# Attention and mixture kernel: VectorE takes the second key tile's turned probabilities out of PSUM

## What is computed

```
h = layernorm(x)
q = rope(rms_norm(h) * q_norm_w)          # 16 heads of width 32
k = rope(rms_norm(ctx) * k_norm_w)        # 4 key heads, each for 4 query heads
v = ctx                                   # 4 value heads
s = where(causal, q @ k.T / sqrt(32), -1e30)
x = x + softmax(s) @ v @ w_out.T
y = layernorm(x)
probs = softmax(y @ w_router); the 4 largest of 128 give each of 8 bases a weight per token
mixed = sum over 8 bases of weight * silu(y @ w_gate) * (y @ w_up)
x = x + mixed @ w_down + (silu(y @ shared_gate) * (y @ shared_up)) @ shared_down
```

## Time and profile before

| | |
|---|---|
| device time, median of 3 runs | 809.68 us (809.2 to 809.68) |
| the profiled execution's own time | 809.42 us |
| its span | 807.7 us |
| TensorE busy | 763.8 us, 95% |
| VectorE busy | 646.1 us, 80% |
| ScalarE busy | 578.0 us, 72% |
| GpSimd busy | 532.5 us, 66% |

### The profile page before, as it was taken

How to read it: one execution, slowest core, us unless ns; L and a number is a source line. 1 busy time by engine, 2 the same in 40 slices (tenths; PEclk the granted TensorE clock), 3 DMA queues, 4 the chain that set the end, 5 groups by cost and what they waited for, 6 DMA issues and landing times. The chain is left out here.

```text
span 807.7 us, 15292 instructions
## 1 busy us (share of the span) xinstructions
PE 763.8 (95%) x4180; PEld 608.0 (75%) x4180; DVE 646.1 (80%) x1635; ACT 578.0 (72%) x1413; POOL 532.5 (66%) x685
## 2 busy tenths in 40 slices
PE   2768799999999999999999999999999999999998
PEld 2545577777777878777778778777778887788886
DVE  7767787889788877889788787888788887688774
ACT  3878796788777867788778767787777775655552
POOL 4586489784697769775687849777465615662572
PEclk9979999999999999999999999999999999999999
DMA  8323144554545446545455445554545335454650
GB/s 291 122 68 97 41 134 161 179 166 138 192 156 172 153 141 220 194 154 178 146 175 179 141 157 181 170 164 135 197 150 173 136 125 185 157 188 133 207 201 35
DMA packets 57052, 127.03 MB, mean 157 GB/s; under 512 B 10920, under 2 KB 28040, under 8 KB 56968
## 3 DMA queue, kind: packets, MB, share of 16 engines
q1 hardware_dynamic: 56968, 126.04, 47.3%
HBM read 107.55 MB, written 4.46 MB: 139 GB/s over the span
## 5 line engine op out<-in xcount | busy, mean ns | idle before, releaser
L1634 PE MATMUL u<-w_h,t_h 128*128 128x512 f32 x640 | 258.4, 404 | 1.1 <-issue 0.8
L1634 PE MATMUL u<-w_l,t_h 128*128 128x512 f32 x640 | 251.2, 393 | 0.0
L1634 PE MATMUL u<-w_h,t_l 128*128 128x512 f32 x640 | 251.0, 392 | 0.0
L1284 DVE TENSOR_TENSOR w_l<-w_raw,w_h 128x512 fp32r<-128x512 f32 x288 | 240.4, 861 | 0.3 <-ACT w_h L945 0.3
L945 ACT ACTIVATE w_h<-w_raw 128x512 fp32r<-128x512 f32 x384 | 219.0, 621 | 7.9 <-DMA w_raw<-in_w_units 7.0
L899 POOL TENSOR_TENSOR w_l<-w_raw,w_h 128x512 fp32r<-128x512 f32 x96 | 139.1, 1449 | 101.8 <-ACT w_h L945 101.8
L980 ACT ACTIVATE scores<-scores,mx 128x384 f32<-128x384 f32 (+1 forms) x224 | 128.8, 575 | 70.4 <-DVE mx L1227 69.2
L907 POOL TENSOR_TENSOR macc<-macc,gb 128x256 f32<-128x256 f32 x112 | 106.1, 951 | 58.9 <-DVE gb L1387 58.4
L1634 PEld LDWEIGHTS u<-w_h,t_l 128*128 128x128 f32 x640 | 120.6, 188 | 26.9
L1227 DVE CUSTOM_DVE_ANT_0 scores<-s,mask_qk 128x384 f32<-128x384 f32 (+1 forms) x224 | 112.4, 503 | 35.5 <-PE s L1510 34.9
L1634 PEld LDWEIGHTS u<-w_h,t_h 128*128 128x128 f32 x640 | 121.0, 189 | 25.8 <-issue 3.0
(11 more groups left out here) (152 smaller groups left out, 1175.0 us busy)
## 6 DMA issues: line engine op xcount, KB each, us to landing
w_raw<-in_w_units SPq DMA_DIRECT2D x160, 512.0 KB, 4.2
w_raw<-in_w_out_t SPq DMA_DIRECT2D x16, 512.0 KB, 5.1
w_raw<-in_shared_w_down SPq DMA_DIRECT2D x16, 512.0 KB, 4.6
q_st<-turned_h SPq DMA_DIRECT2D x224, 32.0 KB, 2.8
out<-x SPq DMA_DIRECT2D x16, 256.0 KB, 2.2
q_st<-turned_l SPq DMA_DIRECT2D x112, 32.0 KB, 2.7
x<-in_x SPq DMA_DIRECT2D x3, 1024.0 KB, 9.2
k_st<-turned_h SPq DMA_DIRECT2D x48, 32.0 KB, 2.8
```

The costliest lines, as they stand in the source:

```text
L1284: e.tensor_tensor(w_l[:, i % WR, k, :], w_raw[:, i % WR, k, :], f32(w_h[:, i % WR, k, :]), ALU.subtract).then_inc(s_wl, 1)
L1634: last = e.matmul(u_bank[n % 2][:], t[:, k, cols], ww[:, i % WR, k, :], start=(k == 0 and m == 0), stop=(k == KC - 1 and m == 2))
```

## The change

In spans 0 to 3 the copy of the second key tile (`k = 1`, 512 columns) goes from ScalarE's queue to VectorE's, as `probabilities_out`, with a semaphore of its own, `s_exv`. It waits for the same transposes. All that waited for the copy (the value product, the next transposes into `pair`) waits for the new semaphore in those four cases. The copies of the first key tile and those of all later spans stay on ScalarE, which now counts four steps fewer.

```diff
+        def exp_out(u, k):
+
+            if u < KV:
+                return (s_exv, u + 1) if k else (s_ex, u + 1)
+            return s_ex, step_no(u, k) - KV + 1
+
         def probable(u, k):
             first = span(u)[1] * TH
             if u < KV or k < first:
-                return s_ex, step_no(u, k) + 1
+                return exp_out(u, k)
...
# GpSimd, mask_probabilities
-                e.wait_ge(s_ex, n + 1)
+                e.wait_ge(*exp_out(u, k))
...
# ScalarE, loop over slots
-                if (step := second_pass_step(s)) is not None:
+                if (step := second_pass_step(s)) is not None and not (step[0] < KV and step[1]):
                     exponential(*step)
...
# VectorE
+            def probabilities_out(u, k):
+                n, width = step_no(u, k), G * (Q - seen(u, k))
+                e.wait_ge(s_pb, n + 1)
+                if n >= PR:
+                    e.wait_ge(s_pv, n - PR + 1)
+                e.tensor_copy(pr[:, n % PR, 0:width], pair[:, 0:width]).then_inc(s_exv, 1)
...
# VectorE, loop over slots
                 for u in value_block(s):
                     attended(u)
+                if (step := second_pass_step(s)) is not None and step[0] < KV and step[1]:
+                    probabilities_out(*step)
                 for g in moments_in(s):
                     moments(g)
...
# TensorE, turn_probabilities and pass_b
-                p_free[0] = (s_ex, step_no(u, k) + 1)
+                p_free[0] = exp_out(u, k)
```

More of the change, by code:

```diff
@@ L226, in attention_and_mixture_kernel @@
             "row_inverse", "inverse_spread", "inverse_turned", "inverse_out"))
-        s_pb, s_ex, s_sel, s_pv = (sem(n) for n in ("pass_b", "exp", "exp_masked", "value_product"))
+        s_pb, s_ex, s_exv, s_sel, s_pv = (sem(n) for n in ("pass_b", "exp", "exp_out_dve", "exp_masked", "value_product"))
         s_att, s_oh, s_ol = sem("attended"), sem("out_high"), sem("out_low")
```

## The result

| | before | changed |
|---|---|---|
| device time, median of 12 runs each | 809.47 us (807.14 to 810.5) | 811.22 us (810.59 to 813.35) |
| ratio, with 95% interval | | 1.0033 (1.0023 to 1.0042) |
| span of the profiled execution | 807.7 us | 809.7 us |
| VectorE busy | 646.1 us | 647.4 us |
| ScalarE busy | 578.0 us | 576.6 us |

The changed kernel is 0.33% slower, 2.7 us (1.9 to 3.4) by the ratio of runs taken side by side, 1.75 us by the two medians. The forecast was 811.7 us, so 2.3 over the profiled execution of before. The changed kernel's median of 811.22 us lies just under the 811.3 that the prediction took as the border to slower; the ratio of runs side by side, whose whole interval lies above 1.002, tells it clearly.

What follows compares the result with a forecast made beforehand. From 30 to 62 us waits between engines bound the kernel, from 100 us TensorE. Steps 1.45 + 0.55 - 0.1 + 0.4 gave +2.3 us over the profiled 809.42, so 811.7 us; range 809.4 to 813.4.

Steps and rivals of the forecast that it cites:

- place 2: Span 1's copy, 39 to 41 us: it runs ahead of the row maximum, lateness grows from 1.45 to 2.0 us.
- place 1: Span 0's copy, 31 to 36 us: copy of 0.66 and moments of 0.88 us make the row maximum 1.45 us late.
- place 3: Span 2's copy, 47 to 50 us: maximum 3.1 us late, but slack at keys and turned_l leaves 1.9 us.
- place 4: Span 3's copy, 58 us: it runs ahead of the row maximum, lateness grows from 1.9 to 2.3 us.
- The copy's price: One 128x512 copy on VectorE: taken as 0.66 us, between ScalarE's 590 ns and the row maximum's 687 ns.
- its second case: Rival, chance 0.27: only the late start of SyncE's query transfers counts, +1.05 us, time 810.5 us.
- The value products: Span 0, sixteen products of 1.51 us at half clock: may fall in a better stretch, taking 0.3 to 0.6 us away.
- the range's first case: VectorE's waits at the four copies delay all behind them: +2.3 us, spanning 1.4 to 2.8 us; chance 0.48.
- ScalarE's relief at nothing: The 2.4 us of copies taken off ScalarE gain nothing, since in spans 0 to 2 it waits next for VectorE.
- the faster case: Rival, chance 0.13: ScalarE decides, each copy gives back up to 590 ns; one gives -0.6 us, all four -2.4 us.
- Carried one for one to the end: From 100 us on TensorE is the bound, so the 2.3 us of delay at 59 us stays to the end.
- The clock: Rival, chance 0.12: more waiting brings TensorE more time at 1.2 GHz, about +1.7 us on top, 813.4 us.

Runs made afterwards that it cites:

- experiment 3: From the changed kernel: each copy on VectorE stands behind the moments of its slot, not ahead of them; 810.84 us, ratio 1.0015 to before.
- experiment 7: From the kernel before: VectorE only waits for the transposes and writes one element of an existing tile, ScalarE keeps the copies; 809.79 us, ratio 1.0005.
- experiment 10: From the changed kernel: only span 0's copy is on VectorE, ScalarE has the other three; 809.80 us, ratio 1.0005 to before.
- experiment 1: From the changed kernel: the four copies are on no engine, value products read the first key tile's probabilities (wrong output); 809.13 us, ratio 0.9992 to before.
- experiment 4: From the changed kernel: each copy one slot later in VectorE's queue, behind the next row maximum and ahead of the inverse; 809.88 us, ratio 1.0008 to before.
- experiment 8: From the kernel before: span 3's queries turned three slots earlier, their transfers right behind; 810.73 us, ratio 1.0016 to before.
- experiment 6: From the changed kernel: the copies of spans 1 to 3 on VectorE, that of span 0 back on ScalarE; 810.61 us, ratio 1.0020 to before.
- experiment 2: From the kernel before: VectorE waits for the transposes and writes 8 elements of a new scratch tile, ScalarE keeps the copies; 813.57 us, ratio 1.0051.

## Why the prediction held

**The mechanism** was a wait put into VectorE's queue ahead of work that others need, and it is what the runs show up to 61 us. Its marks, forecast and found: row maximum behind the first copy 34.05, 33.75; first `q_st` transfer 34.9, 34.62; inverse 35.15, 34.85; maximum of place 2 41.45, 41.45; its inverse 42.5, 42.54; third copy 49.0, 49.07; maximum behind it 50.5, 50.51; first maximum over 384 51.7, 51.76; `turned_l` 52.2, 52.24; last maximum 60.6, 60.29; exponential 61.3, 61.02.

Some of this agreement is luck. The changed kernel's profiled execution was 0.63 us early when the first copies began (its first wide copy at 30.01, that of before at 30.64), and its first transposes then took 1.09 in place of 0.63 us. By the steps, which don't know of the start, the sum stands as follows; place 1 between executions with transposes of the same length, the others as means of two executions each:

| place | forecast | steps, changed - before |
|---|---|---|
| 1 | +1.45 | 8.51 - 6.87 = +1.64; 9.00 - 7.51 = +1.49 |
| 2 | +0.55 | 8.23 - 7.63 = +0.60 |
| 3 | -0.1 | 10.64 - 10.82 = -0.18 |
| 4 | +0.4 | 3.15 - 2.78 = +0.37 |
| sum | +2.3 | +2.3 to +2.4 |

That the sum agrees to 0.1 us is luck as well: step 1 is known to some 0.2 us, and step 3 was 11.06 and 10.57 in the two executions of before, 10.64 in both of the change.

**The copy's price** was taken as 0.66 us and has two values. It is 692 ns long, just above the upper of the two bounds (687), but the next instruction of VectorE starts 0.60 to 0.61 us behind the start of it (32.30 to 32.91, 40.84 to 41.45, 49.07 to 49.67), near the lower (590). What stands behind it feels the second; of the 0.3 us by which the maximum of place 1 came early, 0.2 were there when the copy started. By the table in the Trainium skill (VectorE: DVE Perf Modes, The TRN2 errata) the estimate was 658 ns, between the two; no row here is that long.

**Place 1** was forecast as copy plus moments. Experiments 3, 7 and 10 show both halves: moments first takes it away (6.97), the wait without the copy keeps 0.96 of 1.49, alone it is there in full. In the changed kernel the transfers weren't what passed it on, as the prediction said against its second case: the first maximum over 384 elements, which had waited 0.73 us for TensorE, starts right behind the inverse (51.76). They weren't far off: with place 1 alone TensorE waited 0.96 us for a transfer before 52.80 us.

**Place 2** by the length of the copy holds, and so does **place 3** absorbed by the wait for keys and transfers: with the copy ahead of the last maximum step 3 was 10.38 to 10.78 us in four executions, in the two of before 10.57 and 11.06. The -0.18 of the table is less than that scatter.

**The value products** of place 1 were a term at the low side of the range: 1.51 us as the price of the lower clock, against 0.86, with 0.3 to 0.6 us to be had in a better stretch. That reading doesn't hold. In the changed kernel the granted clock was 1.00 there, and they took 1.51 us again:

```profile
35.02 1.51 PE L1564 MATMUL o_bank<-pr,ct 128*32 128x256 f32 x16
```

```profile
35.00:36.00 1.00, 1.00 (x13) 0.52 (x16) 1.00 (x8) 0.67 (x3) 1.00 (x3) 1.00 0.11 27
```

What decides between the two lengths isn't known. The sum of 2.3 doesn't use this term. The upper end of the range's first case, 2.8, has no term of its own in the prediction.

**ScalarE's relief at nothing** holds within 0.21% by experiment 1. So the faster case falls, for the reason given: the row maximum behind the copy was due within 0.12 to 0.24 us.

**Carried one for one to the end** is right on the whole and too simple for one trace. From the exponential to the first `out<-x` it was 139.8 and 138.2 us in the two executions of before (198.8 - 58.99, and 196.8 - 58.63), 139.8 and 139.9 in those of the changed kernel. From there to the last `out<-x` it was 606.4 and 606.0, against 606.4 and 606.2. So what is lost by 60 us is still lost at 200 and at the end. But a single execution scatters behind 60 us by about as much as the loss: over all runs here but the two with the scratch tile the first stretch took 138.2 to 141.9 us and the second 605.7 to 607.2. The upper values of the first, 141.2 to 141.9, are those of experiments 3, 4 and 8, and it isn't known whether these would show them in each execution. The granted clock drops in varying places in this stretch; that the scatter comes from it was not shown.

**The clock**, a rival with 0.12, isn't decided. Between 50 and 60 us it was 0.66, as before. Between 60 and 70 us it was 0.66 where before had 1.00, and 0.66 again in the second execution, where the second of before had 0.83. But experiment 1, with no copy in VectorE's queue and the total of before, had 0.66 there too:

```profile
60.00:70.00 10.00, 9.44 (x41) 5.92 (x42) 7.97 (x28) 9.64 (x25) 4.90 (x8) 0.66 0.23 57
```

So it isn't shown that more waiting brought more time at 1.2 GHz. The price forecast for it was 1.7 us on top, and that figure doesn't follow from its own terms: two blocks at 0.65 us are 1.3, and as much again for the transposes would be 2.6. The 139.8 and 139.9 us above leave 1.6 and 1.7 us for it against one execution of before, and against the other nothing or 0.1, so 813.4 was an upper end and not the time of that case. Where the clock did read 0.50, in step 4 of experiment 3 (58 to 60 us), the transposes took 1.09 in place of 0.63 us and the step 0.45 us more; but transposes of 1.09 us stand in step 1 at a granted clock of 1.00 as well, so the clock as the profile gives it isn't the whole account of their length.

**What stays open**: which place costs how much of the total, since the totals of experiments 6 and 10 lie the other way round than their steps; and why a write or a wait that makes the distance 1.0 us longer (experiment 7) leaves a total that can't be told from before. Intervals of 0.1 to 0.15% don't settle it.

No version beat the kernel before. Experiments 1, 4, 7 and 10 can't be told from it, and none of them that computes the right result has a reason to be better.

## What to carry to other kernels

An engine with free time isn't a free place for work: in an in-order queue ask what the moved instruction waits for, and what stands behind it. Here the wait of a 0.6 us copy, with 0.9 us of moments behind it that had filled a gap, held up a maximum, a bank, a turned tile and an inverse; with the copy behind the next maximum the loss was too small to measure in the total. And relief of an engine is worth only the idle time that it removes elsewhere: if its next instruction waits for another engine, the relief turns into a longer wait.

## What was not expected of the hardware

A tile of 32 bytes in each partition that nothing touches made the kernel 0.59% slower, more than the whole change. The group of products `u<-w_l,t_h` took 397 in place of 393 and 391 ns, and the time from the first to the last output transfer 610.6 in place of 606.4 us; a second kernel with the same tile (experiment 2) repeats both. That accounts for 2.9 of the 4.2 us by which the time between the transfers grew. The tile shifts the places of all that is allotted behind it; that this, and not the count of tiles, is the cause was only argued. An experiment that adds a tile should be run beside one that adds the tile alone.

An instruction's length in the trace and what it costs its queue differ on VectorE: 692 ns against 0.60 to 0.61 us for the copy, and 0.68 against 0.61 us for a maximum over 512 elements, whose readout starts before the row has ended (52.58 to 53.19 us).
